# Attention scores as 64-row tiles of TensorE, and scores and products two heads at a time in the second attention

## The reference

```python
# first attention: 16 heads of 8 features, rotary embedding, scaled softmax
scores = jnp.einsum('bhqd,bhkd->bhqk', q, k) / jnp.sqrt(jnp.asarray(hd, x.dtype))
attn = jax.nn.softmax(scores, axis=-1)
out = jnp.einsum('bhqk,bhkd->bhqd', attn, v)
...
# second attention: q and k are the same projection; the softmaxed scores are mixed over the heads
scores = jnp.einsum('bhqd,bhkd->bhqk', qk, qk)
a1 = jax.nn.softmax(scores, axis=-1)
a1 = jnp.einsum('gh,bhqk->bgqk', W_x, a1)
o1 = jnp.einsum('bhij,bhjd->bhid', a1, v)
```

## Time and profile before

| | |
|---|---|
| median of 3 runs | 1685.94 us (1684.94 to 1686.06) |
| span of the profiled execution | 1682.3 us |
| between the two | 3.6 us |
| TensorE busy | 97% |
| VectorE, ScalarE, GpSimd busy | 77%, 61%, 57% |
| granted TensorE clock, mean | 0.981 of full speed |

### The profile page before, as it was taken

One profiled execution on the slowest core, in us unless ns is written; L12 is line 12 of the kernel. 1 busy time (PEld: TensorE's weight loads), 2 busy tenths in 40 slices (PEclk: granted clock), 3 DMA queues, 4 the chain that ended last, 5 costly groups with the idle time before them and its releaser, 6 DMA issues. The chain is left out here.

```text
span 1682.3 us, 47420 instructions
## 1 busy us (share of the span) xinstructions
PE 1625.8 (97%) x13660; PEld 1305.6 (78%) x13660; DVE 1302.9 (77%) x3569; ACT 1028.5 (61%) x2372; POOL 961.9 (57%) x1067
## 2 busy tenths in 40 slices
PE   4999999999999989998999999999999999999998
PEld 3566666666666557775999999999999999998997
DVE  5777888888888669987788778877878788884666
ACT  0666767676766756663666666666666666665332
POOL 4444444443444135566778877787778877782222
PEclk7999999999999999997999999999999999999999
DMA  7333333333233100013222222222222221210111
GB/s 211 95 104 101 94 106 95 105 94 109 91 107 94 58 23 28 28 39 93 74 64 74 77 73 63 80 69 78 71 67 71 80 72 63 74 48 17 63 62 53
DMA packets 170158, 128.92 MB, mean 77 GB/s; under 512 B 13036, under 2 KB 143224, under 8 KB 170104
## 3 DMA queue, kind: packets, MB, share of 16 engines
q1 hardware_dynamic: 169136, 127.65, 24.8%
q10 hardware_dynamic: 968, 0.60, 0.1%
HBM read 60.56 MB, written 54.53 MB: 68 GB/s over the span
## 5 line engine op out<-in xcount | busy, mean ns | idle before, releaser
L779 DVE TENSOR_REDUCE shifts<-bank 128x2 bf16<-128x512 f32 x1024 | 699.7, 693 | 186.1 <-PE bank L994 177.5
L723 ACT ACTIVATE probs<-bank 128x512 f32<-128x512 f32 x1024 | 595.1, 594 | 170.2 <-PE bank L983 169.4
L875 PE MATMUL bank<-values,probs 128*128 128x129 f32 x4096 | 541.9, 275 | 0.0
L875 PEld LDWEIGHTS bank<-values,probs 128*128 128x128 f32 x4096 | 497.8, 192 | 7.6 <-issue 0.2
L994 PE MATMUL bank<-k_stack,q_stack 96*128 96x256 bf16 x2048 | 398.2, 276 | 9.3 <-DMA q_stack<-score_parts 5.3
L983 PE MATMUL bank<-q_stack,k_stack 97*128 97x256 bf16 x2048 | 395.8, 274 | 6.5 <-DMA q_stack<-shift_rows 5.3
L581 POOL TENSOR_TENSOR values<-mix,v_in 128x1024 f32<-128x1024 f32 x128 | 301.9, 2359 | 7.6 <-ACT v_in L695 7.6
L590 POOL TENSOR_TENSOR o_odd<-o_odd,scaled 128x256 f32<-128x256 f32 x224 | 162.7, 726 | 164.8 <-ACT scaled L674 164.2
L983 PEld LDWEIGHTS bank<-q_stack,k_stack 97*128 97x128 bf16 x2048 | 180.3, 98 | 91.6 <-ACT probs L723 44.1
L674 ACT ACTIVATE scaled<-bank,recips 128x128 f32<-128x128 f32 x448 | 139.9, 363 | 169.1 <-DVE recips L769 169.1
L994 PEld LDWEIGHTS bank<-k_stack,q_stack 96*128 96x128 bf16 x2048 | 196.2, 98 | 50.3 <-DVE shifts L779 13.6
(11 more groups left out here) (144 smaller groups left out, 2121.3 us busy)
## 6 DMA issues: line engine op xcount, KB each, us to landing
score_parts<-parts SPq DMA_DIRECT2D x128, 192.0 KB, 2.3
k_stack<-score_parts SPq DMA_DIRECT2D x256, 96.0 KB
q_stack<-score_parts SPq DMA_DIRECT2D x256, 96.0 KB
score_parts<-parts SPq DMA_DIRECT2D x128, 128.0 KB, 2.3
score_parts<-parts SPq DMA_DIRECT2D x128, 64.0 KB, 1.8
x_in_f<-x_all SPq DMA_DIRECT2D x64, 128.0 KB, 2.0
x_in<-in_L_attn_x SPq DMA_DIRECT2D x32, 128.0 KB, 3.3
q_stack<-shift_rows SPq DMA_DIRECT2D x256, 2.0 KB
```

What stands on the lines that cost most here:

```text
L723: act.activation(probs[:, s % RING, :, :].rearrange("p t n -> p (t n)"), s2[s % 2][:, :], ACT.Exp, scale=scale).then_inc(exp_done, 1)
L779: dve.tensor_reduce(shifts[:, :, hf, col], s1[s % 2][:, :].rearrange("p (t n) -> p t n", t=TILES), op=ALU.max, axis=AX.X, negate=True).the ...
L875: last = pe.matmul(pv[h % 2][:, q * (D + 1):(q + 1) * (D + 1)], probs[:, h % RING, t, q * P:(q + 1) * P], values[b.odd][:, t, h, :], start ...
```

## The change

The heads' rows now begin at row 0 and at row 64 (`TILE_ROWS`), with the row of ones and maxima behind each (rows 48 and 112). Each score matmul reads 48 rows (first pass) or 49 rows (second pass) of one half of the partitions. `q_stack` has no second copy and no zeros; both stacks stay as large in partitions, `q_stack` is half as large in the free dimension. The first pass now goes over the heads in the order 1, 0, 3, 2, ..., so that in one slot the two passes read opposite halves, and their matmuls alternate. In `attn1` slots go in pairs: scores of two heads, then other work and products of head s-2, other work and products of s-1; VectorE's and ScalarE's orders follow. The DMAs are as many and as large as before. GpSimd sets `k_stack` to one in two instructions instead of four, and VectorE's two for `q_stack` are gone.

```diff
-PAIR_ROWS = 2 * HEAD_ROWS
-SHIFT_ROW = PAIR_ROWS
+TILE_ROWS = 64
+SHIFT_ROW = HEAD_ROWS
...
-        self.q_stack = [sb(f"q_stack{k}", [P, 2, PAIRS, TOK], BF16) for k in range(2)]
+        self.q_stack = [sb(f"q_stack{k}", [P, PAIRS, TOK], BF16) for k in range(2)]
...
+        for stack in core.k_stack:
+            pool.memset(stack[:, :, :], 1.0).then_inc(stacks_set, 1)
...
-        for stack in core.q_stack:
-            dve.memset(stack[:, :, :, :], 0.0).then_inc(q_stacks_set, 1)
...
-    def stack_rows(parity):
-        return slice(parity * HEAD_ROWS, (parity + 1) * HEAD_ROWS)
+    def stack_rows(parity, rows=HEAD_ROWS):
+        return slice(parity * TILE_ROWS, parity * TILE_ROWS + rows)
...
+                if not first and s % 2 == 0 and on(0 if s > 2 else -1):
+                    scale_head(i if s > 2 else i.plus(-1), (s - 3) % HEADS)
                 if on(0):
                     act.wait_ge(s_in_psum, i.number() * HEADS + (s + 1))
...
-                if not first and s % 2 and on(0 if s > 1 else -1):
-                    scale_head(i if s > 1 else i.plus(-1), (s - 2) % HEADS)
...
+                    if first:
+                        max_of_head(i.plus(1), s)
+                    elif s % 2 == 0:
+                        max_of_head(i.plus(1), s)
+                        max_of_head(i.plus(1), s + 1)
+                if not first and s % 2 == 0 and on(0 if s >= 2 else -1):
                     b, h = (i, s - 2) if s >= 2 else (i.plus(-1), s + HEADS - 2)
                     recip_head(b, h)
-                    if h % 2 == 0:
-                        sum_head(b, h)
+                    sum_head(b, h)
+                    recip_head(b, h + 1)
...
+        def scores(i, on, s):
+            if on(0):
+                if s % half_heads == 0:
+                    pe.wait_ge(shifted[s // half_heads], i.number() * 32 + 32)
+
+                wait(pe, exp_done, i.number() * HEADS + (s - 1))
+            if on(1):
+                b = i.plus(1)
+                if s % half_heads == 0:
+                    pe.wait_ge(stacked[s // half_heads], b.number() * 64 + 64)
+
+                wait(pe, max_done, b.number() * HEADS + (s - 1))
+
+            for t in range(TILES):
+                tile = slice(t * P, (t + 1) * P)
+                if on(0):
+                    rows = stack_rows(s % 2, HEAD_ROWS + 1)
+                    score = pe.matmul(s2[s % 2][:, t * TOK:(t + 1) * TOK], core.k_stack[i.odd][rows, s // 2, tile],
+                                      core.q_stack[i.odd][rows, s // 2, :], start=True, stop=True)
+                    if t == TILES - 1:
+                        score.then_inc(s_in_psum, 1)
+                if on(1):
+                    h, b = s ^ 1, i.plus(1)
+                    rows = stack_rows(h % 2)
+                    score = pe.matmul(s1[s % 2][:, t * TOK:(t + 1) * TOK], core.q_stack[b.odd][rows, h // 2, tile],
+                                      core.k_stack[b.odd][rows, h // 2, :], start=True, stop=True)
+                    if t == TILES - 1:
+                        score.then_inc(max_in_psum, 1)
...
         def step(i, on):
             for s in range(HEADS):
+                if not first and s % 2 == 0:
+                    scores(i, on, s)
+                    scores(i, on, s + 1)
...
+                if first:
+                    scores(i, on, s)
...
-        final("sync", late, q_stacks_set=2)
+        final("sync", early, stacks_set=3)
```

More of the change, by code:

```diff
@@ L241, in prepare @@
     late_taken = late.sem("late_taken")
-    q_stacks_set = late.sem("q_stacks_set")
     @early.engine("sync")
@@ L286, in _ @@
         pool.memset(core.zeros[:, :], 0.0).then_inc(stacks_set, 1)
[L287 to L292 removed]
+        for stack in core.k_stack:
+            pool.memset(stack[:, :, :], 1.0).then_inc(stacks_set, 1)
+        pool.wait_ge(stacks_set, 3)
     @late.engine("gpsimd")
@@ L513, in shift_rows_in @@
             for parity in range(2):
-                sp.dma_start(core.q_stack[b.odd][SHIFT_ROW:SHIFT_ROW + 1, parity, 4 * hf:4 * hf + 4, :].rearrange("q r n -> q (r n)"),
+                row = parity * TILE_ROWS + SHIFT_ROW
+                sp.dma_start(core.q_stack[b.odd][row:row + 1, 4 * hf:4 * hf + 4, :].rearrange("q r n -> q (r n)"),
                              shift_rows[hf][4 * parity:4 * parity + 4, :]).then_inc(shifted[hf], 16)
@@ L524, in stack_in @@
                 for side, to in ((0, core.k_stack[b.odd][stack_rows(parity), prs, :]),
-                                 (1, core.q_stack[b.odd][stack_rows(parity), parity, prs, :])):
+                                 (1, core.q_stack[b.odd][stack_rows(parity), prs, :])):
                     src = scratch[side, :, parity * 64:(parity + 1) * 64, :].rearrange(
```

38 lines of the change are left out of this document (6 added, 32 removed).

## The result

The changed kernel takes **1655.95 us** (median, 1652.67 to 1664.07), the kernel before 1685.44 us (1683.15 to 1686.06); the ratio is 0.9835, with an interval of 0.9806 to 0.9863. So it is faster by 1.65%, clear of the noise though under 2%: 29.5 us and not the 88 us that were predicted. The profiled execution has a span of 1650.9 us, against 1682.3.

The account below looks back on a forecast made before the run. TensorE's work was taken to bound both attentions, the stacks' chain close behind in `attn0`. Span 1682.3 - 48 (`attn1`) - 34 - 4 (`attn0`) - 2 (start) = 1594.3 us, with 3.6 around it 1598 us; range 1562 to 1668.

Parts of the forecast that it names:

- What bounds the kernel: Both attentions: TensorE's own work is the bound, with a second bound close behind in `attn0`.
- Change 1, two half arrays: Both attentions: a slot's four score matmuls overlap, 0.23 us instead of 0.44, saving 3.4 us a step.
- Rival D: Both attentions: the two halves do not overlap, a slot's scores stay at 0.44 us; 1784 us, chance 0.10.
- Change 2, the switches: TensorE: each change of array shape costs 0.10 us, +1.6 us a step in `attn1`, +1.1 in `attn0`.
- Rival C: Both attentions: a switch costs 0.2 us, as weight loads of the new shape cannot be made ahead; 1665 us, chance 0.13.
- Change 3, the pairs: `attn1`: the order in pairs fits, except late second exponentials in slots 4 and 5; +0.3 us a step.
- `attn1` together: `attn1`: step from 23.73 to 22.2 us, -1.5 us a step, -48 us over 32 steps.
- The chain in `attn0`: `attn0`: stack loads and part writes, slot 15 to slot 0 two steps on, take 17.6 us; step 16.0, -34 us.
- the last two: `attn0`: the last two steps, which load no stacks, give some 2 us each, -4 us.
- VectorE in `attn0`: `attn0`: some waits of scores on VectorE's maxima come up, +0.2 us a step.
- rival B: `attn0`: the chain of the stacks gives way, step 15.0 us; 1568 us, chance 0.12.
- The start: Start of the kernel: without VectorE's second `q_stack` fill SP goes on 1.8 us earlier, first stacks follow; -2 us.

Follow-up runs that it names:

- e6: The kernel before with two score scratches and the parts written one step earlier, from step 1 on; 1680.99 us, ratio 0.9976.
- e2: The changed kernel with the first pass reading the same half of the partitions as the second in each slot; 1731.69 us, ratio 1.027.
- e9: The changed kernel with two score scratches and the parts in `attn0` written one step earlier, from step 1 on; 1638.12 us, ratio 0.9719.
- e7: The changed kernel with ScalarE scaling the odd head ahead of a slot's copies in `attn1`, not behind them; 1649.91 us, ratio 0.9802.
- e13: The changed kernel with a second score scratch, parts in their old place but not waiting for the second-half load to land; 1645.98 us, ratio 0.977.
- e11: The changed kernel with the turns of the maxima in `attn1` moved from slots 1 and 9 to 2 and 10; 1657.75 us, ratio 0.9825.
- e12: The changed kernel with the edits of e9 (parts a step early) and e7 (ScalarE's scaling earlier) together; 1622.23 us, ratio 0.9626.

## Why the prediction was wrong

The sign was right, and the time lies inside the range; the size was wrong by a factor of three. Point by point:

- **What bounds the kernel**: right. TensorE set both loops, with the chain of the stacks close behind it in `attn0`; in e6, without the chain, the step was only 0.04 us shorter.
- **Change 1, two half arrays** (0.23 us for a slot's scores, -3.4 us a step): right. 0.22 us. Rival D is refuted. The Trainium skill ("TensorE: Matmul & The Clock Gate", LDWEIGHTS) gives the time of one load, and the profile's mean is near it, 94 and 95 ns for the two passes where the rule has 107. What failed is to add four of them up to 0.43 us: the loads of the two halves ran side by side. (The turning point of rival D is mis-stated as well: 1.9 us of switches and waits over 16 slots are 0.12 us a slot, so it lies at 0.32 us and not at 0.35.) e2 shows that the expectation of neighbours that must alternate was too strict.
- **Change 2, the switches** (0.10 each, +1.6 in `attn1`, +1.1 in `attn0`): mis-sized, and the step that failed most. The two rows that I read, scores to products and products to scores, do cost 0.10 each. But the fp32 products get longer by 0.10 behind a switch, between their first and second matmul. In `attn1` the sum was 8 x 0.30 + 2 x 0.10 = 2.6 instead of 1.6 us: **32 us** of the miss. It could have been read ahead, in rows of before that I left unread:

```profile
311.50 1.03 PE L971 MATMUL bank<-x_t,w_qk 128*128 128x256 f32 x4
312.36 0.38 PE L983 MATMUL bank<-q_stack,k_stack 97*128 97x256 bf16 x2
```

Behind scores the projection takes 312.36 - 311.50 = 0.86 us; the same one behind products, where the shape changes, takes 0.97. I had taken the 0.97 for its own cost. In `attn0` the switches came to +1.4 instead of +1.1 (17.13 - 3.5 + 1.4 = 15.05, TensorE's own time in e9's paragraph); a projection beside row tiles (0.59 for 0.44, 0.67 for 0.44) costs up to 0.23 us more. Rival C (0.2 a switch) was nearer in size. Its cause, a weight load that cannot be made ahead, was not tested.
- **Change 3, the pairs** (+0.3 us): mis-sized, 0.65 us, **11 us**. I looked for the wait at the exponentials of slots 4 and 5. It came at the bank of head 1, which ScalarE empties behind its wait for the v projection; I had named that wait as harmless ("such a wait ends near 1.9"), because I followed the copy and the exponential behind it but not the scaling. e7 took it away and got 0.5 us a step back. The rest is the exponential behind the turn of x, which I had put at no cost.
- **`attn1` together**: forecast -48 us, and +32 and +11 and -4 (0.22 instead of 0.23) make -9. Measured -9.5.
- **The chain in `attn0`** (W 14.4, chain 17.6, step 16.0, -34 and -4 for the last two): the mechanism was right, with its place and its mark, the idle time ahead of slot 0. The step was 16.31, and the loop gave 26 us instead of 38. W itself was right, 14.41 in the undisturbed steps, but with some luck: the switches cost 0.3 more, the scores 0.1 less, and the 0.2 put down for VectorE did not show. The chain was 0.2 us too short, 17.8 where it bound, which is 0.1 us a step. I had explained its pace by the landing of a load, 3.5 us; e13 shows that this landing is 0.7 us of it, and that SP's issuing holds the larger part. The step is half of W and that distance together, (14.41 + 17.8) / 2 = 16.1; the other 0.2 us up to 16.31 is the half clock after the longer waits, which I had at nothing. In one such stretch, 315.00 to 317.86, TensorE took 2.86 us for what takes 0.57 + 1.06 = 1.63 at the full clock: 1.2 us lost, and four such stretches make some 5 us. What is left of the 12 us, some 3 to 4, was not traced; it lies in the first and last steps of the loop, outside the average.
- **VectorE in `attn0`** (+0.2 us): in the changed kernel hidden by the chain; e9 shows it at 0.8 us once the chain is gone, so rival B's 15.0 us was out of reach with VectorE's order as it is (15.83).
- **The start** (-2 us): wrong. SP did go on earlier (18.91 us for 20.24), but the issue of `x_in`, now right behind those of x_all, took 3.44 us and not 2.23:

```profile
18.91 3.44 SPq L533 DMA_DIRECT2D x_in<-in_L_attn_x  x1
```

The parts were issued at 22.40 us, 0.1 us earlier than before. And TensorE stayed at the half clock to 58.2 us, where before it was at the full one from 51.8, so that the first products came 2.3 us later:

```profile
52.00:58.00 6.00, 6.00 (x28) 3.02 (x28) 2.89 (x5) 2.03 (x5) 0.00 (x0) 0.50 0.56 166
```

Why the clock rose later there was not tried. The start is 4.3 us of the miss; the stretches outside the two loops are 1.8 more. What also stays open is the variation of `attn0` from one execution to the next (16.3 to 16.9 us a step among kernels that share its code). It goes with the half-clock stretches: the changed kernel's profile has four, that of e7 eight and that of e11 twelve, while those of e9 and e12 have none. Within one stretch the order is plain: the wait comes first and the clock falls after it. In e11 the stretches then come every 34 us, two steps, from 218 to 525 us, and the chain offers a reason: a step at the half clock is 1.5 us longer, slot 0 behind it has nothing to wait for, and the slot 0 after that waits the longer (1.1 to 2.4 us in the changed kernel). What starts such a series in one execution and not in another is open.

## What to carry to other kernels

Here two row tiles halved the time of matmuls with a short contraction, but each change of the array's shape back to fp32 products was paid twice: at the switch, and again in the first fp32 matmuls behind it. Count round trips and read their price from full rows on both sides, not from the gap alone; then group work of one shape. When the bounding engine gets faster, look for the chain that lies next to it, follow every instruction of the issuing queue in it, and of each engine that waits in a new order, follow all that stands behind the wait, releases of buffers above all. And when a mean step is off, list the steps one by one: here most of them were as forecast, and a few were not.

## What the runs showed of the hardware

- Two 64-row tiles with weight loads of 128 bf16 columns ran at twice the rate of the whole array: 0.055 us a matmul of 256 columns instead of 0.11.
- A round trip into row tiles and back to fp32 over the whole array cost 0.30 us, of which 0.10 us between the first and the second fp32 matmul (0.21 us apart instead of 0.11). The Trainium skill, "TensorEngine Tiling (Array Packing)", Key Properties, says that a change of the tiling mode drains the engine; it gives no price, and the rows agree that a switch costs time.
- The queued matmuls of one half started beside earlier ones of the other (e2: eight in 0.55 us, switch included, with the halves four by four).
- After waits of 1.6 to 2.4 us in the loop of the changed kernel TensorE was granted the 1.2 GHz level for a few microseconds (0.55 in 314.5 to 318); with waits of 0.3 us it stayed at the 2.4 GHz level (e9, 1.00). Long waits were not always followed by it: after 1.67 and 1.58 us in e13 (at 165.7 and 356.9 us) the granted clock stayed at 1.00.
